# Rider edges of a graph layer: h rows out of the selecting product, destination rows as one f32 product, and pairs of chunks in one VectorE operation

## The reference

```
h = relu(_ln(x @ W1 + b1, g1, bt1))
row, col = (edge_index[0], edge_index[1])          # source, destination of each edge
h_src = h[row]
ef = concatenate([h_src, h[col]], axis=1)
edge_weights = sigmoid(relu(ef @ We1 + be1) @ We2 + be2)[:, 0]
aggr = segment_sum(edge_weights[:, None] * h_src, col, num_segments=n)
gate = sigmoid(concatenate([h, aggr], axis=-1) @ Wg + bg)
out = _ln(gate * aggr + (1.0 - gate) * h, g2, bt2)
```

## Time and profile before

| | |
|---|---|
| median of three runs | 2202.27 us (2200.88 to 2204.13) |
| the profiled execution's own span | 2389.9 us |
| mean granted TensorE clock in it | 0.671 |
| PE, PEld, DVE, ACT, POOL busy, us | 1789.8, 1600.5, 1786.0, 1145.9, 1443.2 |

### The profile page before, as it was taken

How to read it: one execution, slowest core, us unless ns; L and a number is a source line. 1 busy time by engine, 2 the same in 40 slices (tenths; PEclk the granted TensorE clock), 3 DMA queues, 4 the chain that set the end, 5 groups by cost and what they waited for, 6 DMA issues and landing times.

```text
span 2389.9 us, 41229 instructions
## 1 busy us (share of the span) xinstructions
PE 1789.8 (75%) x13028; PEld 1600.5 (67%) x13029; DVE 1786.0 (75%) x4120; ACT 1145.9 (48%) x2984; POOL 1443.2 (60%) x1430
## 2 busy tenths in 40 slices
PE   4989885764554688888898898887877887777880
PEld 3777775543554577777787788876767776676750
DVE  7777774958985788887888887788787776776656
ACT  1555543755440355554555554555554444444325
POOL 4444410557776666666666666666666666666645
PEclk9999997886665555555555655567666566667665
DMA  7888984054334455455545455555555555555411
GB/s 270 290 289 290 314 296 148 27 175 147 115 119 136 121 145 155 146 153 149 154 144 154 146 160 157 169 158 163 156 166 160 168 154 166 163 162 164 134 35 54
DMA packets 278501, 392.65 MB, mean 164 GB/s; under 512 B 74753, under 2 KB 178436, under 8 KB 278155
## 3 DMA queue, kind: packets, MB, share of 16 engines
q1 hardware_dynamic: 216979, 226.19, 29.9%
q0 software_dynamic: 57024, 155.79, 22.1%
q10 hardware_dynamic: 4280, 8.03, 1.0%
HBM read 374.69 MB, written 15.12 MB: 163 GB/s over the span
## 4 chain that ended last, share of the span: by engine, by line
PE 62%; issue 18%; DVE 7%; POOL 5%; ACT 3%; DVEq 2%; DMA 1%; ACTq 1%; another core or an unknown queue 0%; SPq 0%; POOLq 0%
PE bank L556 15%; PE bank L1414 10%; PE bank L1437 8%; PE bank L1416 7%; PE bank L503 7%; PE bank L532 5%; POOL x_rows L922 3%; PE bank L1445 3%; PE bank L1303 2%; PE bank L1392 2%; ACT ring L1018 1%; DVE stats L1773 1%; POOL ring L922 1%; DMA dst_table<-ring 1%; PE bank L511 1%
## 5 line engine op out<-in xcount | busy, mean ns | idle before, releaser
L922 POOL DMA_INDIRECT x_rows<-src_table,lane_src x892 | 886.8, 994 | 441.3 <-issue 242.6
L1414 PE MATMUL bank<-ring,sums 128*128 128x128 f32 x980 | 336.0, 428 | 74.7 <-issue 73.5
L922 POOL DMA_INDIRECT ring<-src_table,lane_src x296 | 293.0, 990 | 144.1 <-issue 79.9
L1416 PE MATMUL bank<-ring,sums 128*128 128x128 bf16 x1470 | 258.3, 285 | 145.2 <-issue 143.3
L560 DVE TENSOR_TENSOR sums<-sums,bank 128x128 f32 (+4 forms) x812 | 201.4, 248 | 220.1 <-issue 142.2
L556 PE MATMUL bank<-weighted,x_rows 128*128 128x40 f32 x1784 | 328.2, 361 | 10.8 <-issue 10.8
L556 PEld LDWEIGHTS bank<-weighted,x_rows 128*128 128x128 f32 x1784 | 326.7, 281 | 11.0 <-issue 10.9
L1416 PEld LDWEIGHTS bank<-ring,sums 128*128 128x128 bf16 x1470 | 175.0, 133 | 196.3 <-issue 176.1
L1414 PEld LDWEIGHTS bank<-ring,sums 128*128 128x128 f32 x980 | 236.5, 290 | 88.4 <-issue 87.5
L542 DVE SCALAR_TENSOR_TENSOR bank<-bank,we_all 128x512 f32<-128x512 f32 x421 | 278.0, 693 | 15.4 <-PE bank L1416 3.6
L1909 DVE TENSOR_SCALAR sums<-sums,ring 128x64 f32<-128x64 f32 (+3 forms) x490 | 141.8, 357 | 194.3 <-remote 194.1
(11 more groups left out here) (252 smaller groups left out, 3092.6 us busy)
## 6 DMA issues: line engine op xcount, KB each, us to landing
ring<-in_edge_attr SPq DMA_DIRECT2D x195, 512.0 KB, 5.1
ring<-rel_table SPq DMA_DIRECT2D x74, 512.0 KB
ring<-cell_table SPq DMA_DIRECT2D x121, 256.0 KB
ring<-src_table SPq DMA_DIRECT2D x144, 128.0 KB
x_rows<-src_table,lane_src POOLq DMA_INDIRECT x892
ring<-dst_table SPq DMA_DIRECT2D x297, 32.0 KB
ring<-src_table SPq DMA_DIRECT2D x104, 64.0 KB
src_table<-ring SPq DMA_DIRECT2D x12, 512.0 KB, 3.7
```

Source lines behind the costliest of these rows:

```text
L922: eng.indirect_dma_start(gathered(c)[:, j, :], None, src_table, bass.IndirectOffsetOnAxis(ap=lane_src[:, t:t + 1], axis=0)).then_inc(gathe ...
L1414: eng.matmul(o, src_hot[:, u % 2, e], src_part[:, u % U_SLOTS, col_block(u, i), :], start=True, stop=False, skip_group_check=True)
L1416: last = eng.matmul(o, dst_hot[:, u % 2, e], base_dst[:, k % 2, s, :], start=False, stop=(s == PARTS - 1), skip_group_check=True)
```

## The change

1. A rider's load takes whole rows of `src_table` (`node_part`, source part and h). The f32 product that selects source parts is 256 columns wide and yields the h rows of the cells as well (`cell_both`: `cell_hidden` and `cell_h`). ACT copies `cell_h` out of PSUM (`rows_out`). `cell_sums_mm` multiplies these rows by the weighted destination one-hot, straight into `folded_out`. `h_load`, `fold`, `sums_out` and the two steps' lag are gone.
2. The three bf16 parts of a class's destination rows are summed once (`base_sum`, in four of the steps) into an f32 `base_dst`; a rider's column is then one f32 product of 128 columns with an f32 one-hot in place of three bf16 ones.
3. PSUM is one tensor, and the two banks of a pair lie side by side: `add_src_part` and both operations of `edge_dots` are done once a pair, on 1024 columns. `window_out` and `folded_out` have one bank and no second, so `wsum(q)` needs `acc2(q - 1)`; DVE's `acc2` stands ahead of `logits`.
4. ACT makes the destination one-hots ahead (`places`, three slots); DVE's `cell_weigh` is one operation for all columns and doesn't need `wsum(q - 2)` any more. ACT takes both sigmoids of a step in one operation, and both cell one-hots likewise.
5. In the sort, stationary and moving operand change places: one product of 256 columns a token (two in class 0) where there were two of 98 (196).

`rider_mm` now also needs `cell_rows` of the rider before: ACT's copy, which itself needs that rider's `cell_logit` (DVE) and `wsum(q - 2)` (PE).

```diff
-        def edge_dots(eng, parts):
-
-            for _, hid, n in parts:
-                eng.scalar_tensor_tensor(hid[:, 0:n, :], hid[:, 0:n, :], 0.0, wide["we2"][:, :].unsqueeze(1).to_broadcast([P, n, P]),
-                                         ALU.max, ALU.mult)
+        def edge_dots(eng, out, hid):
+
+            n = hid.shape[1]
+            eng.scalar_tensor_tensor(hid, hid, 0.0, wide["we2"][:, :].unsqueeze(1).to_broadcast([P, n, P]), ALU.max, ALU.mult)
             eng.drain()
-            for out, hid, n in parts:
-                last = eng.tensor_reduce(out[:, 0:n], hid[:, 0:n, :], AX.X, ALU.add)
-            return last
+            return eng.tensor_reduce(out, hid, AX.X, ALU.add)
...
-            return bank[(0, 1, 2, 6)[i % 4]][:, :].rearrange("p (j f) -> p j f", j=J)
+            return bank[i % 4].rearrange("p (j f) -> p j f", j=J)
+
+        def hidden_pair(q):
+            first = 2 * (q % 2)
+            return psum[:, first:first + len(pair_chunks(q)), :].rearrange("p c (j f) -> p (c j) f", j=J)
 
         def window_out(i):
-            return bank[3 + i // 2 % 2][:, i % 2 * W0:i % 2 * W0 + W]
+            return bank[6][:, i % 2 * W0:i % 2 * W0 + W]
+
+        folded_out = bank[6][:, P:2 * P]
...
+        cell_both = psum[:, 4:6, :].rearrange("p b (k f) -> p (b k) f", f=2 * P)
+        cell_hidden, cell_h = cell_both[:, :, 0:P], cell_both[:, :, P:2 * P]
...
             def rider_load(u):
                 k, blocks = riders_of[u]
                 need(eng, "rider_hidden", u - U_SLOTS)
-                rows_ = src_table[blocks[0] * P:(blocks[-1] + 1) * P, 0:P]
-                eng.dma_start(src_part[:, u % U_SLOTS, 0:len(blocks), :], rows_.rearrange("(b p) f -> p b f", p=P)).then_inc(rider_in[u % U_SLOTS], 16)
+                rows_ = src_table[blocks[0] * P:(blocks[-1] + 1) * P, :]
+                eng.dma_start(node_part[:, u % U_SLOTS, 0:len(blocks), :], rows_.rearrange("(b p) f -> p b f", p=P)).then_inc(rider_in[u % U_SLOTS], 16)
...
-            def sums_out(q):
-
+            def rows_out(q):
                 u = riders[q]
-                need(eng, "wsum", q)
-                for i in range(len(riders_of[u][1])):
-                    last = eng.activation(pair_weight[u % 2][i][:, 0:span(u)], weight_out(q, i)[:, 0:span(u)], ACT.Copy)
-                last.then_inc(done("pair_weight"), 1)
+                n = rider_cols(u)
+                need(eng, "cell_logit", u)
+                need(eng, "wsum", q - 2)
+                eng.activation(cell_rows[:, u % 2, 0:n, :], cell_h[:, 0:n, :], ACT.Copy).then_inc(done("cell_rows"), 1)
...
+                    eng.activation(place[u % PLACES][:, i, 0:span(u)], iota_s[:, 0:span(u)], ACT.Abs, bias=cell_dst[:, at_ + i:at_ + i + 1], scale=-1.0)
+                eng.drain()
+                hot_ = place[u % PLACES][:, 0:n, 0:span(u)]
+                eng.activation(hot_, hot_, ACT.Relu, bias=ones[:, 0:1], scale=-1.0).then_inc(done("place"), 1)
...
             need(eng, "hot_t", 0)
             for q in range(1, 3):
                 sort_columns(q)
             for q in range(n_steps):
+                if q in riders:
+                    rows_out(q)
                 edge_weight(q)
-                if q - 2 in riders:
-                    sums_out(q - 2)
-                if q in riders:
-                    place_sources(q)
+                if q + 1 in riders:
+                    places(q + 1)
...
-                for i, t in enumerate(sort_tokens(q)):
-                    for v in range(2):
-                        eng.matmul(cell_sums(k, v), rows_[:, i, v, :], cols_[:, i, :],
-                                   start=(t == first and v == 0), stop=(t == end - 1), skip_group_check=True)
...
                 need(eng, "cell_logit", u - 1)
+                need(eng, "cell_rows", u - 1)
                 if u == first_rider[k]:
-                    loaded(eng, "base_dst", k + 1)
+                    need(eng, "base_dst", k)
                 eng.wait_ge(rider_in[u % U_SLOTS], 32 * (u // U_SLOTS + 1))
                 eng.wait_ge(done("cell_hot"), u + 1)
                 for i in range(rider_cols(u)):
-                    o = cell_hidden[:, i, :]
                     e = slice(i * P, (i + 1) * P)
-                    eng.matmul(o, src_hot[:, u % 2, e], src_part[:, u % U_SLOTS, col_block(u, i), :], start=True, stop=False, skip_group_check=True)
-                    for s in range(PARTS):
-                        last = eng.matmul(o, dst_hot[:, u % 2, e], base_dst[:, k % 2, s, :], start=False, stop=(s == PARTS - 1), skip_group_check=True)
+                    eng.matmul(cell_both[:, i, :], node_hot[:, u % 2, 0, e], node_part[:, u % U_SLOTS, col_block(u, i), :], start=True, stop=False, skip_group_check=True)
+                    last = eng.matmul(cell_hidden[:, i, :], node_hot[:, u % 2, 1, e], base_dst[:, k % 2, :], start=False, stop=True, skip_group_check=True)
...
-                need(eng, "place_src", u)
-                cap = CLASSES[riders_of[u][0]][2]
-                for i in range(rider_cols(u)):
-                    eng.matmul(weight_out(q, col_block(u, i))[:, 0:span(u)], place_src[:, u % 2, i, :], place_dst[:, u % 2, i, 0:span(u)],
-                               start=(i % cap == 0), stop=(i % cap == cap - 1), skip_group_check=True)
-
-            def fold(u, q):
-                k, blocks = riders_of[u]
-                eng.wait_ge(h_in[u % U_SLOTS], 16 * (u // U_SLOTS + 1))
-                eng.wait_ge(done("pair_weight"), u + 1)
-                for i, b in enumerate(blocks):
-                    eng.matmul(folded_out(q)[:, 0:span(u)], h_part[:, u % U_SLOTS, i, :], pair_weight[u % 2][i][:, 0:span(u)],
-                               start=(i == 0), stop=(b == blocks[-1]), skip_group_check=True)
+                need(eng, "cell_rows", u)
+                n = rider_cols(u)
+                for i in range(n):
+                    eng.matmul(folded_out[:, 0:span(u)], cell_rows[:, u % 2, i, :], place[u % PLACES][:, i, 0:span(u)],
+                               start=(i == 0), stop=(i == n - 1), skip_group_check=True)
 
             def wsum(q):
                 need(eng, "weigh", q)
-                need(eng, "acc2", q - 2)
-                if q in folded:
-                    fold(folded[q], q)
+                need(eng, "acc2", q - 1)
                 if q in riders:
                     cell_sums_mm(riders[q], q)
...
+            def base_sum(k):
+
+                loaded(eng, "base_parts", k + 1)
+                eng.tensor_tensor(base_dst[:, k % 2, :], base_parts[:, k % 2, 0, :], base_parts[:, k % 2, 1, :], ALU.add)
+                for s in range(2, PARTS):
+                    eng.drain()
+                    last = eng.tensor_tensor(base_dst[:, k % 2, :], base_dst[:, k % 2, :], base_parts[:, k % 2, s, :], ALU.add)
+                last.then_inc(done("base_dst"), 1)
...
             def cell_weigh(u, q):
                 n = rider_cols(u)
-                at_ = rider_cells(u)
-                for i in range(n):
-                    eng.tensor_scalar(place_dst[:, u % 2, i, 0:span(u)], iota_s[:, 0:span(u)], cell[:, 1, at_.start + i:at_.start + i + 1],
-                                      cell_weight[:, q % 4, i:i + 1], ALU.is_equal, ALU.mult)
+                need(eng, "place", u)
+                hot_ = place[u % PLACES][:, 0:n, 0:span(u)]
+                eng.tensor_tensor(hot_, hot_, weight[:, q % 4, 2, 0:n].unsqueeze(2).to_broadcast([P, n, span(u)]), ALU.mult)
 
             def logits(q):
                 if q in riders:
                     u = riders[q]
                     need(eng, "weight", q - 4)
                     need(eng, "rider_hidden", u)
-                    edge_dots(eng, [(cell_logit[:, q % 4, :], cell_hidden, rider_cols(u))]).then_inc(done("cell_logit"), 1)
+                    edge_dots(eng, logit[:, q % 4, 2, 0:rider_cols(u)], cell_hidden[:, 0:rider_cols(u), :]).then_inc(done("cell_logit"), 1)
                 need(eng, "hidden", q)
                 for j in range(2):
                     eng.wait_ge(gather_in[q % (G_SLOTS // 2)][j], 32 * sum(len(pair_chunks(i)) for i in range(q % (G_SLOTS // 2), q + 1, G_SLOTS // 2)))
-                for c in pair_chunks(q):
-                    add_src_part(eng, hidden(c), gathered(c))
+                n = len(pair_chunks(q))
+                add_src_part(eng, hidden_pair(q), gathered_pair(q))
                 need(eng, "weight", q - 4)
                 eng.drain()
-                edge_dots(eng, [(logit[:, q % 4, c % 2, :], hidden(c), J) for c in pair_chunks(q)]).then_inc(done("logit"), 1)
+                edge_dots(eng, logit[:, q % 4, 0:n, :].rearrange("p c j -> p (c j)"), hidden_pair(q)).then_inc(done("logit"), 1)
...
-                    need(eng, "wsum", q - 2)
                     cell_weigh(riders[q], q)
...
-            run_stages(n_steps, [(0, hot_t), (3, weigh_), (2, logits), (5, acc2)])
+            run_stages(n_steps, [(0, hot_t), (3, weigh_), (5, acc2), (2, logits)])
```

140 lines of the change are left out of this document (62 added, 78 removed).

## The result

The changed kernel takes 2208.38 us (median of 7 runs, 2206.87 to 2218.76) beside 2202.10 of the kernel before (2199.59 to 2205.23): ratio 1.0041, interval 1.0025 to 1.0057. The ratio is taken from all runs; that of the two medians alone is 1.0029. By the medians the change costs 6 us. The time lies inside my range, but I had given "slower" 0.28 and forecast 52 us of gain.

What follows compares the result with a forecast made beforehand. POOL's 10.12 us a step was taken as the floor, with DVE and PE rounds close by; only POOL's remaining wait could be won, 60.5 x 124/149 = 50 us, so 2202 - 50 = 2152, said as 2150; own range 2125 to 2180, overall 2090 to 2290.

Steps and rivals of the forecast that it cites:

- The step that failed: POOL's "remote" waits of 248.1 us, less 187.6 taken as the profile's own, leave 60.5 us of waiting.
- 1502.3 us: POOL's own work: gathers of 1179.8 us plus 322.5 us of "issue" ahead of them, 10.12 us a step.
- The second step that failed: wsum's new wait on PE for DVE's acc2 of the step before: priced at 0, upper bound 0.5 us a step.
- An operation on 1024 columns: DVE: six operations on 512 columns become three on 1024, at 1.22 us each; each merge saves 0.07 us.
- the merged weighing: DVE: four weighings of 1.15 us together become one of 0.43 to 0.69 us, saving 0.62 us.
- DVE's saving: DVE's round gets 0.83 us a step shorter, 103 us of DVE's time.
- A rider's column at half clock: PE: f32 products of 256 and 128 columns take 1.28 us a column, up from 0.85; +1.72 a rider.
- The copy: ACT's copy of h rows, between earlier sums and the next rider, adds 0.72 us to PE's round, bounds 0.5 to 1.0.
- A (more is won): POOL's gap before each gather is partly the profile's own, so DVE's 103 us comes through: 2099 us; chance 0.13.
- B (nothing happens): Something shared by PE and POOL sets the pace, or copy and new wait take DVE's gain: 2202 us; chance 0.09.
- C (slower, by the late signal): Rider waits for ACT's copy, which waits for PE's late window-sums signal: about 2310 us at 2.5 us lateness; chance 0.21.
- D (the clock stays at half): PE's clock stays at half, its round 12.43 us: +265 us, about 2415; chance 0.07.

Runs made afterwards that it cites:

- experiments 1 to 4 and 16: Changed kernel with register loads late, loads spread, copy early, loads spread and copy early: 2409.57, 2396.40, 2414.85, 2394.57 us; kernel before with loads spread: 2391.59.
- Experiment 9: Changed kernel with DVE loading two window starts in every step, behind acc2, instead of 16 every eighth step ahead of it: 2188.56 us, ratio 0.9941.
- Experiments 7 and 8: Kernel before and changed kernel, each with half of POOL's gathers: 2129.61 and 2120.27 us.
- experiment 14: Changed kernel with half of the gathers, no copy of the h rows by ACT, and two register loads a step behind acc2: 2094.70 us.
- experiment 8: Changed kernel with half of POOL's gathers: 2120.27 us.
- experiment 5: Kernel before, unchanged, timed and traced again: 2200.84 us, with a trace span of 2199.4.
- experiment 1: Changed kernel with DVE's 16 register loads behind the additions of acc2 instead of ahead of them: 2409.57 us, ratio 1.0010.
- experiment 16: Kernel before with its register loads spread, two a step behind acc2: 2391.59 us, ratio 0.9987.
- Experiment 17: Changed kernel with half of the gathers, two register loads a step behind acc2, and ACT's copy kept: 2108.84 us.

## Why the prediction was wrong

**The step that failed** is "Then POOL still waits 248.1 - 187.6 = 60.5 us", on which the forecast rests. Two errors are in it. First, the 187.6 us were not the profile's own. They belong to conditions under which the kernel before takes some 2400 us in its timed runs too (experiments 1 to 4 and 16) and 11.9 us a step, so waits of that trace could not be set off against a time of 2202. Second, I counted POOL's work as 1502.3 us with the "issue" of those gathers only that waited for nothing. Every gather has its 0.305 us; for the 131 that waited in that trace (322.5 us of "issue" are 1057 gaps of 0.305, of 1188) it lay hidden in the wait. The floor is 1179.4 + 1187 x 0.305 = 1541 us, and 131 x 0.305 = 40 us of my 60.5 were never to be had. What was left is the 18.3 us that the new trace of before shows: the most that the change could win at this floor, where I forecast 50. Experiment 9 leaves 4.9 of it, and is 13 us faster than the kernel before. Experiments 7 and 8 show that the loop gets shorter once the gathers are fewer.

**The second step that failed**: "the wait falls at a time when PE is at the rider or the sort; I price it at 0, with 0.5 us a step as the upper bound (62 us)". The place was right for most steps. In every eighth, 3.27 us of register loads stand ahead of the awaited additions. By experiment 9 the wait with the loads in it costs 20 us, inside the bound, but I had taken the wrong end. That is why the time rose and did not merely stay. The loads were to be seen in the page of before, among 142.2 us of "issue" ahead of L560.

**The sizes that held.** An operation on 1024 columns takes 1.22 to 1.23 us (predicted 1.22), the merged weighing 0.42 to 0.69 (0.43 to 0.69). Groups of DVE in after:

```profile
L540 DVE TENSOR_TENSOR psum<-psum,x_rows 128x1024 f32<-128x1024 f32 x111 | 136.0, 1226 | 57.5 <-DMA x_rows<-src_table,lane_src 57.4
...
L1893 DVE TENSOR_TENSOR sums<-sums,weight 128x256 f32<-128x256 f32 x33 | 13.7, 416 | 0.0
L1893 DVE TENSOR_TENSOR sums<-sums,weight 128x512 f32<-128x512 f32 x16 | 11.0, 685 | 1.3 <-ACT weight L1126 1.3
```

DVE's saving is 88 us between 800 and 2100 us, some 0.7 a step (0.83 predicted). It went into waiting. Over the loop that is for gathered rows (78.2 us ahead of L540; ahead of L537 before 61.2) and for the rider's products (62.1, none before), and from 800 to 2100 us the "issue" ahead of L560 grew from 81.7 to 94.0. An engine behind a floor shows it so: its saving comes back as waiting. A rider's column at half clock, from the timeline of PE:

```profile
943.09 1.06 PE L1397 MATMUL psum<-ring,sums 128*128 128x256 f32 x2
...
944.37 1.06 PE L1397 MATMUL psum<-ring,sums 128*128 128x256 f32 x2
```

That is 1.28 us, as predicted. The copy holds PE for 0.79 us here and 0.82 on average (99.3 us in 121 waits; 0.72 predicted).

**The rivals.** A (more is won): no. POOL's 0.305 us is in every trace, and experiment 5 shows a trace to be as long as its run, so the gap is no surcharge of the profile. B (nothing happens) comes nearest in time, but the slowdown is clear of noise. With all gathers its causes are not the ones; with half of them the second is near: experiment 14, without copy and without loads ahead of `acc2`, is 35 us under the kernel before with half, where experiment 8 is 9 us under it. C (slower, by the late signal) does not hold in this trace: the copy starts at 940.98, 0.10 us after the last window sum ends at 940.88, and taking it away gives some 2 to 6 us. D (the clock stays at half): no, it is 0.78. That it is above the 0.61 that I asked for says little, since the kernel before has 0.71 here, not the 0.60 of the earlier trace rows. The slowdown is by a mechanism that I had listed and not made a rival.

**The two chips with 2403 to 2405.** On both, POOL's waits end by "remote" in traces of kernels with all gathers, as in the earlier trace rows: in experiment 1 (the first chip) 111 of them from 800 to 2200 us, 1.9 us each, and in experiment 16 (the second) 100 from 800 to 2000. Experiment 17, with half of the gathers, ran at 2108.84 on the second chip, its waits end by PE's window sums, and the copy starts 0.10 us after the sums (1218.45 after 1218.35). So the signal was late there only with all gathers. What makes it late is not settled. Nor is it settled that the chip is the cause, since no chip was measured under both conditions; nor rival C there, since the changed kernel itself was not run on them.

## What to carry to other kernels

Before a wait is counted as gain, compute the floor of the engine that waits: the number of its instructions times the busy time of one plus its gap, with the gaps that lie hidden in waits counted too. When a change makes an engine wait for a nearer step, look at what stands ahead of the awaited instruction on the other engine, register loads included: they show only as "issue", and in few steps. When a trace is much longer than the runs (here by 187.6 us), it is of other conditions: take it again beside its own run before any row of it is set against the runs' time. All later traces were within 3 us of theirs.

## What was not expected of the hardware

A gather on POOL takes longer beside some operations of DVE. In the trace of after, the 621 gathers beside which DVE ran only operations that read or write PSUM took 0.948 us on average, the same as the 103 with DVE idle. The 53 in whose middle the merged weighing L1893 ran, whose operands all lie in SBUF, took 1.17. Over the loop the mean is 0.993: up to 1188 x 0.045 = 53 us of POOL's floor may be contention with DVE. No run here took it away, so that is an estimate and not shown.

The load of 16 values into DVE's registers took 3.27 us and that of two 0.50, in neither case with an instruction in the profile.
